# Dynamics buffers given on at the second state step, and a new order of steps on every engine, in a four-layer kernel on one Trainium2 core

## The chip, the cores and the metric

The kernel runs on one core of a Trainium2 chip. The metric is the time of one execution on the device in microseconds (us), all of it: loading the inputs and the weights, the arithmetic and the store of the result. Lower is better. Engines are named as in the profile: PE is TensorE's matmul, PEld its weight load, DVE VectorE, ACT ScalarE, POOL GpSimd, SP SyncE (here it only issues loads).

## The reference, cut to what matters

An input of 8 x 256 tokens of width 128 (float32) goes through four layers. Each layer is a mixer and then a feed-forward stage, each followed by a residual sum and a normalisation:

- layer 0: a complex decaying convolution along the sequence; then 8 experts of which each token uses 2 (hidden width 256)
- layer 1: causal attention with rotary positions (2 heads of 64), with an output projection; then attention with 4 heads on shared keys and values, and 8 + 1 experts (hidden width 128)
- layer 2: attention in a window of 32 (16 heads of 8); then the "dynamics": two iterations of a small state machine, and a refinement
- layer 3: attention of the 32 keys back of which the 16 highest scores count, with a mean over the phrase; then 8 experts (hidden width 342)

The dynamics, to which the change belongs, in short:

```python
probs = softmax(gelu(xf @ router_w1 + b) @ router_w2 + b); topk_p, topk_i = top_k(probs, 2)   # the readout
v, s = 0, xf
for _ in range(2):
    ctx = concat([s, v])
    shared_ctrl = gelu(ctx @ shared_w1) @ shared_w2
    ctrl = for each chosen expert: gelu(ctx @ w1[e]) @ w2[e]
    x_next, v_next = _inl(...)           # sigmoid, softplus, sigmoid of the three parts of the controls
    halt = sigmoid(gelu(s @ halt_w1) @ halt_w2)
    s, v = s + halt * (x_next - s), v + halt * (v_next - v)
out = xf + integration_weight * (gelu(s @ refine_w1) @ refine_w2)        # the refinement
```

## The kernel before

The tokens are cut into four chunks of 512 (two sequences each). Every chunk goes through nine stages: A (convolution), B (experts of layer 0), C, D1 (the two attentions of layer 1), D2 (its experts), E (window attention), F (dynamics), G (phrase attention), H (experts of layer 3). 0F is stage F of chunk 0. A stage is cut into ticks; 0F[12] is its tick 12. Per engine the ticks of one chunk have a fixed order, and the order in which the four chunks' steps are woven together stands in a string of digits per engine (`MERGE`): each digit is the chunk whose next step is written out now. `interleave` reads it. Each engine runs its instructions in the order written and waits on semaphores where it needs another engine's result. A second string, `BANK_OF`, says for each step of PE which of the 8 PSUM banks it writes; before a bank is written again, PE waits for its last reader (`begin`).

What the chunks share is taken in turns (`TURNS`): the `att` buffers (16 tiles of 512 columns, for A, C, D1, E, G), the ring of expert weights and hidden tiles (`w_exp` with 4 slots, `hid` with 6, for B, D2, H), and the `dyn` buffers (16 tiles, for F). For `att` the turns are 0A 1A 2A 3A 0C 0D1 1C 1D1 0E 2C 2D1 1E 3C 3D1 0G 2E 1G 3E 2G 3G; for the ring 0B 1B 0D2 2B 1D2 3B 2D2 3D2 0H 1H 2H 3H; for `dyn` 0F 1F 2F 3F. `take(region, k, stage)` waits for what `released` returns: for `att` after A and D1 the normalisation, else the residual sum; for F too the residual sum, which is its last tick but two (F[55]). So chunk k+1 can't write its first tile of `dyn` before chunk k's refinement is done.

An expert of B takes four 128x512 products on PE (L450, gate and up, two halves) and eight of 128x128 (L485, down); in D2 two and four, in H six and twelve. ACT applies SiLU to the gate (L1820, L1818), DVE multiplies with the up part (L1195, L1192) and adds the weighed result to `x` (L1209, the mix), and only then are the banks free. SP loads the next expert's weights when an older one's down product is done.

Stage F on PE: F[2] and F[4] are the readout (router), F[9] turns the one-hots of the two chosen experts over, F[12] spreads their weights (32 rows), `step(k, n, i)` for n = 0, 1 is a state step: six hidden products (L780), the halt (i = 7, 32 rows), the shared controls (i = 8, L792, 64 rows), eight products that pick the weights of the chosen experts (i = 9 to 12, bf16, 32 rows), the slots' bias (L747, 32 rows) and controls (L757). F[49] to F[54] are the refinement, F[55] to F[57] on DVE and POOL the residual sum and the normalisation. In H, POOL computes a square root by a power (L2180) for the routing.

## Time and profile before

| | us |
|---|---|
| median of 3 runs | 1227.08 |
| lowest, highest | 1224.92, 1227.92 |
| the profiled execution, whole | 1226.56 |
| span of the profiled instructions | 1224.5 |
| PE busy | 1115.4 (91%) |
| DVE, ACT, POOL busy | 827.1, 657.6, 219.1 |
| mean granted clock of PE | 0.959 |

The profile is of one execution. Its times count from the first instruction. In the timeline a row merges instructions of one line that follow each other; on PE a float32 product counts as two. "PEclk" is the granted clock: 1.00 is 2.4 GHz, 0.50 is 1.2 GHz, a mean between them says how much of a stretch lay at either. Two kinds of loss on PE add up: time in which it waits, and time in which it works at half clock.

### The profile page before, as it was taken

The numbers are of one execution on the slowest core, as the hardware profiler recorded it, in microseconds if no ns is written. First come the engines' busy times: TensorE is split into PE (matmuls) and PEld (weight loads), VectorE is DVE, ScalarE is ACT, GpSimd is POOL, SyncE is SP. The second block draws the span as 40 slices with busy tenths as digits, with TensorE's granted clock in tenths as the row PEclk, the third lists the DMA queues.
The fourth block names the chain that finished last, engine by engine and source line by source line (L and its number), as shares of the span: only waits on it lengthen the run. The fifth ranks groups of instructions, "written<-read, shape, count | busy, mean of one in ns | idle before, by whom it ended". The sixth has DMA issues, their size and how long they took to land.

```text
span 1224.5 us, 16730 instructions
## 1 busy us (share of the span) xinstructions
PE 1115.4 (91%) x5800; PEld 629.4 (51%) x5800; DVE 827.1 (68%) x2446; ACT 657.6 (54%) x1028; POOL 219.1 (18%) x251
## 2 busy tenths in 40 slices
PE   0799967799999999999799989999999999999996
PEld 0455544566554455554455555454464553565554
DVE  6987566489577369868486696678584774664534
ACT  0225344555756766677666575668546655542321
POOL 1312042224021214131200150005020000202000
PEclk9899989899989989997899999799999999999999
DMA  7021100121110000001001111001001010111210
GB/s 268 4 73 54 39 14 14 30 68 34 33 48 24 27 14 21 20 27 33 1 14 56 37 37 37 1 18 37 18 28 37 18 37 1 45 36 54 79 56 9
DMA packets 45394, 45.91 MB, mean 37 GB/s; under 512 B 2584, under 2 KB 44192, under 8 KB 45056
## 3 DMA queue, kind: packets, MB, share of 16 engines
q1 hardware_dynamic: 42336, 40.59, 10.9%
q10 hardware_dynamic: 2976, 4.26, 1.0%
q8 instruction: 47, 0.77, 0.2%
q14 instruction: 35, 0.29, 0.1%
HBM read 43.79 MB, written 1.05 MB: 37 GB/s over the span
## 4 chain that ended last, share of the span: by engine, by line
PE 77%; DVE 13%; ACT 4%; DMA 3%; issue 2%; POOL 1%; POOLq 0%; DVEq 0%; ACTq 0%
PE bank L450 32%; PE bank L485 13%; PE bank L757 10%; PE bank L780 5%; ACT L1781 2%; PE bank L457 2%; PE bank L525 2%; PE bank L439 2%; PE bank L747 1%; PE bank L792 1%; PE bank L668 1%; DMA xt<-x_in 1%; DVE x L1209 1%; DMA w_exp<-in_ffn 1%; PE bank L508 1%
## 5 line engine op out<-in xcount | busy, mean ns | idle before, releaser
L450 PE MATMUL bank<-xt,w_exp 128*128 128x512 f32 (+1 forms) x784 | 390.6, 629 | 19.1 <-DMA w_exp<-in_ffn 6.4
L1781 ACT ACT_TABLE_LOAD x186 | 238.6, 1283 | 70.9 <-PE bank L450 41.7
L450 PEld LDWEIGHTS bank<-xt,w_exp 128*128 128x128 f32 (+1 forms) x784 | 134.5, 190 | 193.7 <-issue 117.1
L485 PEld LDWEIGHTS bank<-w_exp,hid 128*128 128x128 f32 (+1 forms) x1568 | 189.3, 196 | 52.2 <-issue 15.8
L485 PE MATMUL bank<-w_exp,hid 128*128 128x128 f32 (+1 forms) x1568 | 199.0, 282 | 5.7 <-DVE hid L1192 4.2
L1209 DVE SCALAR_TENSOR_TENSOR x<-bank,dense,x 128x128 f32<-128x128 f32 x384 | 107.9, 343 | 119.4 <-PE bank L485 103.0
L757 PE MATMUL bank<-picked,w_dyn 128*128 128x512 f32 x320 | 142.9, 596 | 0.0
L1818 ACT ACTIVATE hid<-bank,w_cols 114x512 f32<-114x512 f32 x96 | 65.2, 687 | 114.6 <-PE bank L450 114.0
L2187 POOL TENSOR_SCALAR rstd<-mv 128x4 f32<-128x4 f32 x32 | 7.0, 218 | 552.6 <-DVE mv L1075 552.4
L1820 ACT ACTIVATE hid<-bank 128x512 f32<-128x512 f32 x100 | 57.5, 597 | 85.1 <-PE bank L450 84.7
L757 PEld LDWEIGHTS bank<-picked,w_dyn 128*128 128x128 f32 x320 | 59.1, 190 | 74.8 <-issue 74.7
L2271 POOL TENSOR_TENSOR att<-att,lsm 128x512 f32<-128x512 f32 x64 | 67.8, 1075 | 140.7 <-DVE lsm L1415 130.1
L1192 DVE SCALAR_TENSOR_TENSOR hid<-bank,w_cols,hid 114x512 f32<-114x512 f32 x96 | 70.3, 745 | 27.4 <-PE bank L450 21.1
L1195 DVE TENSOR_TENSOR hid<-bank,hid 128x512 f32<-128x512 f32 x100 | 66.7, 681 | 17.9 <-ACT hid L1820 14.6
L525 PE MATMUL bank<-w_const,att 128*128 128x128 f32 x304 | 45.2, 283 | 12.0 <-DVE hid L1195 3.6
L1844 ACT COPY att<-bank 128x512 f32<-128x512 f32 (+1 forms) x80 | 41.1, 581 | 20.9 <-PE bank L525 20.9
L525 PEld LDWEIGHTS bank<-w_const,att 128*128 128x128 f32 x304 | 35.7, 145 | 30.8 <-issue 12.7
L780 PE MATMUL bank<-xt,w_dyn 128*128 128x512 f32 (+2 forms) x96 | 49.8, 617 | 1.1 <-DVE xt L1531 1.0
L1555 DVE TENSOR_TENSOR picked<-dyn,bank 128x512 f32<-128x512 f32 x64 | 39.5, 679 | 10.3 <-PE bank L450 10.3
L2202 POOL TENSOR_TENSOR att<-att,rowsum 128x512 f32<-128x512 f32 x32 | 32.8, 1051 | 74.5 <-DVE rowsum L1250 74.5
L1793 ACT ACTIVATE xt<-bank 128x512 f32<-128x512 f32 x24 | 14.3, 594 | 58.3 <-PE bank L439 58.3
L1085 DVE TENSOR_SCALAR x<-x,mv,rstd 128x128 f32<-128x128 f32 x112 | 32.5, 353 | 14.3 <-POOL rstd L2188 14.2
(288 smaller groups left out, 1515.9 us busy)
## 6 DMA issues: line engine op xcount, KB each, us to landing
w_exp<-in_ffn SPq DMA_DIRECT2D x68, 192.0 KB, 3.2
w_exp<-in_ffn SPq DMA_DIRECT2D x32, 384.0 KB, 3.5
w_exp<-in_ffn SPq DMA_DIRECT2D x32, 342.0 KB, 3.1
w_dyn<-in_dyn ACTq DMA_DIRECT2D x1, 1636.0 KB, 12.1
w_const<-in_const SPq DMA_DIRECT2D x1, 1274.0 KB, 11.7
xt<-x_in SPq DMA_DIRECT2D x4, 256.0 KB, 15.4
out<-x ACTq DMA_DIRECT2D x4, 256.0 KB, 2.3
att<-in_stage SPq DMA_DIRECT2D x1, 512.0 KB, 5.2
```

Source lines behind the costliest of these rows:

```text
L450: nc.tensor.matmul(seqs(bk[0:rows, :]) if len(rhs.shape) == 3 else bk[0:rows, :], lhsT, rhs, start=True, stop=True).then_inc(S[k % STREAMS ...
L485: last = nc.tensor.matmul(bk[:, t * 128:(t + 1) * 128], hid[0:rows, (e * nf + f) % RING_H, t * 128:(t + 1) * 128], ffn_w(k, st, "down", e, ...
L525: last = nc.tensor.transpose(bk[:, o:o + 128], a(u)[:, i * 128:(i + 1) * 128], ident)
L757: last = nc.tensor.matmul(bk[:], part("dyn", "ex_w2")[:, h * 384 + at:h * 384 + at + 128], picked[:, 2 * h + t - 1, :], start=False, stop= ...
L780: last = nc.tensor.matmul(seqs(bk[0:rows, :]), lhs, src, start=(half == 0), stop=(half == len(use) - 1))
L1192: V.scalar_tensor_tensor(o, u, col("b1", j, rows), o, ALU.add, ALU.mult).then_inc(X.hidden.s, 1)
L1195: V.tensor_tensor(o, u, o, ALU.mult).then_inc(X.hidden.s, 1)
L1209: last = V.scalar_tensor_tensor(x[:, s, t, :], bk[:, t * 128:(t + 1) * 128], dense[:, s, t, ex:ex + 1], x[:, s, t, :], ALU.mult, ALU.add)
L1781: A.preload_act_table_set(name)
L1818: A.activation(dst, src, ACT.Silu, bias=col("bg", j, rows)).then_inc(X.silu.s, 1)
L1820: A.activation(dst, src, ACT.Silu).then_inc(X.silu.s, 1)
L2271: G.tensor_tensor(v, v, spread(lsm[:, u, row, :], 2, 64), op).then_inc(done, 1)
```

## The change

It has two parts.

First, stage F. The readout's hidden tile, the one-hots and the three tiles of the refinement no longer lie in the shared `dyn` buffers but in the chunk's own `nx` (`flat(s)`) and, for the first refinement tile, in its own `xt`. So `take("dyn", k, "F")` moves behind F[4], and the region is given on at the second state step (`X.stepped`), not at the residual sum. The first state step starts one tick later. Since two chunks can now be in F at once, the engines that raise one semaphore for several chunks get a wait for the previous count (`in_turn`, and one on DVE); each is for an earlier instruction of the same engine.

Second, all the digits of `MERGE` and `BANK_OF` are new: the steps of each engine stand in another order. No step is added or taken away; on ACT the new order has 178 table loads among the steps where the old one has 186. `TURNS` and `TICKS` are as they were.

```diff
 MERGE = dict(
     PE=(
-        "0000000100000011200000000003200000000000000000000231111111101000001100111111101010101010111111111111"
...
+        "0000000000000100000000000001001000000002000000220111111111113011111100000110011111100100110101111111"
...
             if u in ("A", "D1"):
                 return S[q].normed, (q, {"A": "a", "D1": "d2"}[u])
+            if u == "F":
+                return X.stepped, (q, 1)
             return S[q].resid, (q, u)
...
-        oh3 = y(F_CTRL)[:, 0:TILES * 3 * 4 * E8].rearrange("p (t r e) -> p t r e", t=TILES, r=3)
+        def one_hots(s):
+            return flat(s)[:, 0:TILES * 3 * 4 * E8].rearrange("p (t r e) -> p t r e", t=TILES, r=3)
+
+        def refining(s, j):
+            return xtv(s) if j else seqs(flat(s))
...
                     if i == 2:
-                        take("dyn", k, "F")
                         pe.wait_ge(T.xt_ready.s, T.xt_ready.at(k, "F"))
...
                     if i == 4:
                         pe.wait_ge(X.ro_hid.s, X.ro_hid.at(k))
-                        by_token(k, ("F", "logits"), lambda t: y(F_VEL)[0:32, t * 128:(t + 1) * 128],
+                        by_token(k, ("F", "logits"), lambda t: flat(s)[0:32, t * 128:(t + 1) * 128],
                                  part("dyn", "ro_w2")[0:32, :], E8, (T.logits, (k, "F")))
                         yield
+                        take("dyn", k, "F")
...
-                    yield from step(k, 0, i - 3, bks)
+                    yield from step(k, 0, i - 4, bks)
...
-                        take("dyn", k, "F")
...
+                        if X.oh_ready.at(k) > 1:
+                            dve.wait_ge(X.oh_ready.s, X.oh_ready.at(k) - 1)
...
+            def in_turn(sg, *event):
+
+                if sg.at(*event) > 1:
+                    act.wait_ge(sg.s, sg.at(*event) - 1)
...
-                        A.activation(y(F_REF + j), T.bank(k, "F", "ref", j)[:], ACT.Gelu,
+                        in_turn(X.ref, k, j)
+                        A.activation(refining(s, j), seqs(T.bank(k, "F", "ref", j)[:]), ACT.Gelu,
```

The lines of the changed kernel lie 5 further on (L450 is L455 there, L485 is L490, L1195 is L1200).

First place, DVE near the start: the convolution of chunk 2 (L1261 to L1280) and what stands around it. Before:

```order
L1195 TENSOR_TENSOR hid<-bank,hid 128x512
L1085 TENSOR_SCALAR x<-bank,mv,rstd 128x128 x4
L1261 TENSOR_TENSOR att<-xt,inject 128x512
L1263 SCALAR_TENSOR_TENSOR att<-sc,att 128x256 x2
L1271 SCALAR_TENSOR_TENSOR att<-sc,att 128x256 x2
L1275 TENSOR_TENSOR att<-att,turn 128x512
L1276 TENSOR_TENSOR att<-xt,att 128x512
L1280 TENSOR_TENSOR att<-att 128x512
L1195 TENSOR_TENSOR hid<-bank,hid 128x512
```

The same place in the changed kernel, again from the end of chunk 1's stage A on:

```order
L1200 TENSOR_TENSOR hid<-bank,hid 128x512 x2
L1090 TENSOR_SCALAR x<-bank,mv,rstd 128x128 x4
L1266 TENSOR_TENSOR att<-xt,inject 128x512
L1268 SCALAR_TENSOR_TENSOR att<-sc,att 128x256 x2
L1214 SCALAR_TENSOR_TENSOR x<-bank,dense,x 128x128 x4
L1200 TENSOR_TENSOR hid<-bank,hid 128x512 x2
L1276 SCALAR_TENSOR_TENSOR att<-sc,att 128x256 x2
L1280 TENSOR_TENSOR att<-att,turn 128x512
L1281 TENSOR_TENSOR att<-xt,att 128x512
```

What moved: expert work of chunk 0 (hidden tiles and a mix) now stands between the two halves of chunk 2's scans, and the end of chunk 3's stage A stands behind all of 0B and behind six hidden tiles of 1B, where before only half of 0B stood ahead of it.

Second place, PE in the first state step of chunk 2's dynamics (2F), from its shared controls (L792) to its slot bias. Before:

```order
L792 MATMUL bank<-dyn,w_dyn 128x512 x2
L450 MATMUL bank<-kt,w_const 128x512 x2
L450 MATMUL bank<-ohb,slot_b 128x512 x8
L450 MATMUL bank<-xt,w_exp 114x512
L747 MATMUL bank<-kt,w_dyn 128x512 x2
L450 MATMUL bank<-xt,w_exp 114x512 x2
```

In the changed kernel:

```order
L797 MATMUL bank<-dyn,w_dyn 128x512 x2
L455 MATMUL bank<-xt,w_exp 114x512
L455 MATMUL bank<-ohb,slot_b 128x512
L455 MATMUL bank<-xt,w_exp 114x512
L455 MATMUL bank<-ohb,slot_b 128x512
L455 MATMUL bank<-xt,w_exp 114x512
L455 MATMUL bank<-ohb,slot_b 128x512 x2
L455 MATMUL bank<-xt,w_exp 114x512
L455 MATMUL bank<-ohb,slot_b 128x512
L455 MATMUL bank<-xt,w_exp 114x512
```

What moved: the eight picking products (`ohb,slot_b`, 32 rows) stood in one block; now full-height products of 0H stand between them.

Third place, PE near the end: the last product of 3G (`att`) and the start of 3H. Before:

```order
L935 MATMUL bank<-att 128x128
L450 MATMUL bank<-xt,w_exp 114x512 x6
L485 MATMUL bank<-w_exp,hid 128x128 x12
L439 MATMUL bank<-w_const,x 128x128 x4
L949 MATMUL bank<-sc,w_const 128x8
L450 MATMUL bank<-xt,w_exp 114x512
L457 MATMUL bank<-w_rows,xt 128x8 x4
L450 MATMUL bank<-xt,w_exp 114x512 x5
L485 MATMUL bank<-w_exp,hid 128x128 x12
```

In the changed kernel:

```order
L940 MATMUL bank<-att 128x128
L490 MATMUL bank<-w_exp,hid 128x128 x12
L974 MATMUL bank<-w_b,nx 128x128 x4
L444 MATMUL bank<-w_const,x 128x128 x4
L954 MATMUL bank<-sc,w_const 128x8
L462 MATMUL bank<-w_rows,xt 128x8 x4
L455 MATMUL bank<-xt,w_exp 114x512 x12
L490 MATMUL bank<-w_exp,hid 128x128 x12
```

What moved: between 3G's last product and 3H's turning over (L439, now L444) stood half an expert's six products and twelve down products, and then five experts of 2H before 3H's own experts; now it is the last down products of 2H and the bias product, and 3H follows at once.

## Rows read from the trace of the kernel before

**Rows 1.** The page: busy time of each engine.
```profile
PE 1115.4 (91%) x5800; PEld 629.4 (51%) x5800; DVE 827.1 (68%) x2446; ACT 657.6 (54%) x1028; POOL 219.1 (18%) x251
```
**Rows 2.** Stretches: start:end, length, busy (x instructions), granted clock, DMA share, GB/s.
```profile
0.00:104.50 104.50, 65.59 (x271) 39.27 (x271) 84.80 (x293) 23.02 (x34) 21.13 (x25) 0.97 0.33 109
104.50:170.20 65.70, 57.96 (x363) 37.83 (x363) 41.36 (x141) 34.34 (x84) 18.26 (x26) 1.00 0.13 37
170.20:248.40 78.20, 59.21 (x321) 36.68 (x321) 43.78 (x156) 34.00 (x85) 19.38 (x29) 0.89 0.09 28
248.40:1146.70 898.30, 864.42 (x4549) 477.39 (x4549) 622.86 (x1755) 546.46 (x797) 157.96 (x168) 0.96 0.10 30
1146.70:1224.50 77.80, 68.24 (x300) 38.27 (x300) 34.33 (x104) 19.73 (x28) 2.40 (x4) 0.97 0.14 42
```
**Rows 3.** Timeline of PE, 34 to 80 us: start, length, idle before and releaser.
```profile
34.65 1.84 PE L457 MATMUL bank<-w_lat,xt 128*128 128x8 f32 x8 [0.84 <-ACT xt L1793]
...
49.48 1.03 PE L457 MATMUL bank<-w_lat,xt 128*128 128x8 f32 x8 [0.78 <-ACT xt L1793]
55.03 1.12 PE L439 MATMUL bank<-w_const,att 128*128 128x128 f32 x4 [4.52 <-DVE att L1280]
...
76.17 2.04 PE L485 MATMUL bank<-w_exp,hid 128*128 128x128 f32 x16
78.06 3.76 PE L450 MATMUL bank<-xt,w_exp 128*128 128x512 f32 x8
...
104.49 3.67 PE L450 MATMUL bank<-xt,w_att 128*128 128x512 f32 x8
```
**Rows 4.** Timeline of DVE, 32 to 47 us: stage A of chunk 1, a router, a hidden tile.
```profile
32.70 0.69 DVE L1261 TENSOR_TENSOR att<-xt,inject 128x512 f32<-128x512 f32 x1
...
40.05 0.18 DVE L1144 COPY small<-bank 128x32 f32<-128x32 f32 x1
...
43.25 0.88 DVE L1072 BATCH_NORM_STATS2 stats<-bank 128x6 f32<-128x128 f32 x4
44.17 0.38 DVE L1075 BATCH_NORM_AGGREGATE mv<-stats 128x2 f32<-128x6 f32 x4
44.47 0.66 DVE L1195 TENSOR_TENSOR hid<-bank,hid 128x512 f32<-128x512 f32 x1
46.04 1.37 DVE L1085 TENSOR_SCALAR x<-bank,mv,rstd 128x128 f32<-128x128 f32 x4 [0.91 <-POOL rstd L2188]
```
**Rows 5.** Timeline of PE in 1D1, 222 to 250 us.
```profile
225.56 1.66 PE L450 MATMUL bank<-xt,w_exp 128*128 128x512 f32 x2 [2.44 <-ACT att L1835]
...
246.89 1.06 PE L554 MATMUL bank<-w_lat,att 128*128 128x128 f32 x8
248.37 1.95 PE L450 MATMUL bank<-xt,w_exp 128*128 128x512 f32 x4 [0.42 <-DVE x L1209]
```
**Rows 6.** Stretches at half clock inside F of chunks 0 to 3, columns as in rows 2.
```profile
335.20:342.00 6.80, 6.80 (x14) 2.91 (x13) 1.88 (x3) 3.96 (x6) 0.00 (x0) 0.50 0.00 0
567.30:581.00 13.70, 11.90 (x40) 5.29 (x41) 10.94 (x24) 10.75 (x23) 5.24 (x6) 0.50 0.00 0
775.60:792.70 17.10, 17.10 (x26) 4.99 (x25) 8.08 (x13) 8.46 (x11) 0.00 (x0) 0.50 0.01 1
963.30:966.70 3.40, 3.40 (x6) 1.41 (x5) 3.17 (x6) 0.95 (x1) 0.00 (x0) 0.50 0.00 0
```
**Rows 7.** Timeline of PE in 2F, 774 to 787 us.
```profile
774.94 3.21 PE L792 MATMUL bank<-dyn,w_dyn 64*128 64x512 f32 x4
778.07 3.78 PE L450 MATMUL bank<-kt,w_const 32*128 32x512 f32 x4
781.65 3.88 PE L450 MATMUL bank<-ohb,slot_b 32*128 32x512 bf16 x8
```
**Rows 8.** Timeline of PE, 600 to 611 us: 3D1's projection, then 0G.
```profile
600.95 1.05 PE L554 MATMUL bank<-w_lat,att 128*128 128x128 f32 x8
608.49 2.08 PE L876 MATMUL bank<-w_const,x 128*128 128x128 f32 x8 [6.48 <-DVE nx L1096]
```
**Rows 9.** Timeline, all engines, 1105 to 1118 us: from 3G to the start of 3H.
```profile
1105.30 1.12 DVE L1680 SCALAR_TENSOR_TENSOR x<-bank,small,x 128x128 f32<-128x128 f32 x4 [1.29 <-PE bank L935]
...
1109.77 1.10 DVE L1085 TENSOR_SCALAR x<-x,mv,rstd 128x128 f32<-128x128 f32 x4
...
1110.87 2.94 PE L485 MATMUL bank<-w_exp,hid 114*128 114x128 f32 x24
...
1117.31 5.42 POOL L2180 TENSOR_TENSOR small<-small,expo 128x32 f32<-128x32 f32 x1 [8.19 <-DVE small L1711]
```
**Rows 10.** Timeline of PE, 1142 to 1147 us: the end of 2H.
```profile
1142.47 2.92 PE L485 MATMUL bank<-w_exp,hid 114*128 114x128 f32 x24 [1.97 <-DVE hid L1192]
1145.31 1.15 PE L969 MATMUL bank<-w_b,nx 8*128 8x128 f32 x8
```

100 lines of the change are left out of this document (50 added, 50 removed).

## The prediction

> **What bounds the kernel now.** Read the page's busy line first [rows 1]: PE is busy in 91% of the span, DVE in 68%, ACT in 54%. PE is what everything else feeds, so the question is never how long an instruction on DVE or ACT takes, but whether PE has something to do meanwhile, and at which clock. Then the stretches [rows 2]. Up to 104.5 us PE is busy for 65.6: 27 us pass before its first product can start, and some 12 more in waits. From 104.5 to 170.2 it idles 7.7 us, from 170.2 to 248.4 it idles 19.0 us at a mean clock of 0.89. The long middle, 898 us, has 33.9 us of idle time, under 4%. The last 78 us are chunk 3's experts alone. So a new order can win in three places: the first 250 us, the half clock, and a few single waits; the middle leaves little.
>
> **Part one, stage F's buffers.** It removes no instruction. The waits it adds are for an earlier instruction of the same engine, which is done long before; I cost them at nothing, and they would cost at most 16 times the 0.1 us or so that lies between dependent DVE rows [rows 4], under 2 us. What it gives is freedom: the readout of chunk k+1 can run beside the end of chunk k. In the trace of before no wait on PE for the `dyn` buffers is seen, since the old order put experts there. So this part alone is worth nothing; it counts through the order that it permits.
>
> **Part two, the start.** Before, DVE does all four stages A almost in one piece, and PE waits for chunk 2's at 50.5 us, 4.52 us long, beside 0.84 and 0.78 and two smaller ones: about 7 us, and 6.8 us at half clock after it, 3.4 us lost [rows 3]. In the new order PE has twelve steps of 0B before chunk 1's A, and the DVE work of 0B stands between the scans. This wait goes. But what does the chain of attentions gain? 0C may not touch `att` before 3A is normalised. DVE's sum up to there in the new order: 32.6 us (the end of 0A's scaling, just before the group's first row), then three stages A of 7.35 + 1.26 + 1.37 = 10.0 us each [rows 4], three routers of 3.2, weights 2.5, 22 hidden tiles of 0.65, nine mixes of 1.1 and one normalisation of 2.4: 30.0 + 9.6 + 2.5 + 14.3 + 9.9 + 2.4 = 68.7, together 101.3, with small waits 103. PE's own sum to the same point: from 35.5 us 47 products of 0.9 and ten down groups of 1.9 [rows 3], 42.3 + 19.0, and 8 for transposes, routers and stalls, gives 105. Both say that 0C's projections start at 105 us, and today they start at 104.49 [rows 3]. The chain gains nothing at the start. PE is ahead by some 8 us of 1B, but 1B is also what fills 0D1, so at the end of 0D1 both kernels have done the same work: gain about 1 us, from the SiLU of 1B which no longer comes between 0D1's exponentials on ACT, against one router that now does on DVE.
>
> Next, 1D1. Before, nine experts of 0D2 are all that PE can weave in, and it idles between its products: 2.44 us at 225.6, and so on, until 2B starts at 248.37 [rows 5]. In the new order 0D2 is finished earlier and eleven steps of 2B stand before 1D1's projection: ten products of 0.9 and one down group of 1.9, 10.9 us [rows 3]. They have 19.0 us of idle time to go into [rows 2]. From there on PE is nearly full, so what it is ahead it keeps. **Start: -11 us**, between 0 (the chain becomes later by as much) and -19 (all the idle time of the stretch goes).
>
> **Part two, the clock.** Inside the first state step of F, PE falls to half clock in all four chunks: 6.8, 13.7, 17.1 and 3.4 us, 41.0 in all [rows 6], and half of such a time is lost if PE would have had work, 20.5 us. In the longest one PE was busy throughout [rows 6]; what it did before and in it were products of 64 and 32 rows, one after the other for 10.6 us [rows 7]. In the new order 2F's picks alternate one by one with full-height products of 0H, and 1F's partly with 2D2; 0F's and 3F's blocks stay nearly whole. If the spells of 1F and 2F shrink from 30.8 to about 12 us, 9 us come back. **Clock: -9 us**, between 0 and -20.
>
> Here a rule speaks against me. The row shows a fall without any idle time before it [rows 6]. The Trainium skill, "TensorE: Matmul & The Clock Gate", section "HAM oscillation — how this bites in real kernels", tells of falls that come after PE has idled; by it alone the order of F's products would change nothing, and the sum would be 9 us higher. I go with the row.
>
> **Part two, single waits.** 0G waits 6.48 us for 3D1's last normalisation [rows 8]. The new order puts four steps of 2D2 ahead of it, 3.6 us, and 3D2's transposes. **-4 us**, between 0 and -6.5.
>
> **Part two, the end.** Before, 41 us of 2H follow 3G's last product, from 1105.2 to the first product of 3H behind the row of 1145.31. In the new order only 2H's last down group (2.9) and bias product (1.15) [rows 10] stand between it and 3H. The chain from T, the end of 3G's product: residual sum and statistics 2.4, then on DVE first 2H's mix and sum (which wait for PE, to T + 4.9), scaling 1.1, transposes 0.6, ACT 0.6, logits 1.0: 3H's first product at T + 8.4, in place of T + 5.5 by PE's own work, 2.9 us idle. Then 3H's router waits for POOL's power of 5.42 us [rows 9] on DVE, and five hidden tiles queue behind it; PE can write six halves ahead (10.4 us) before its first down group needs them at T + 20: 2 to 3 us more, and a spell at half clock, 1.7. Against that, today's wait of 1.97 [rows 10] goes. **End: +6 us**, between +1 and +15 (if banks stop PE sooner).
>
> **The middle.** 33.9 us of idle time less 0G's; the new order has other waits. I see no reason for a balance either way: 0, give or take 10. ACT's eight table loads less are 10 us of an engine that is half idle, 0 on PE.
>
> Sum: -11 - 9 - 4 + 6 = -18 from the profiled execution's 1226.6 gives 1208.6; the median of the runs lies 0.5 above that execution, so 1209.
>
> **The rivals.** (a) The clock stays: the spells only move, as idle time elsewhere brings new ones. For it: the stretch with the most idle time, 19.0 of 78.2 us, also has the lowest clock, 0.89 [rows 2], so idle time costs clock as well. 1209 + 9 = 1218. (b) The chain is late: DVE reaches the end of 3A later than 103 us. For it: my sum has it fully busy for 70 us, in fixed order. Each microsecond is one on the attention chain until 1D1; at 114 us the first term is gone, 1220. (c) The orders are equal in what they cover and only the places of the waits change; part one does nothing: 1225. (d) The middle gets better by a third of its idle time too: 1198. (e) **Slower:** the weaving is too fine. The new PE order has 704 rows of equal instructions in place of 649, 55 more changes from one chunk to another; each one that finds its bank still held by a DVE step (0.66 us, the hidden tile) [rows 4] costs PE that much. If more than 33 of them do (18 + 3.7 over 0.66) the kernel is slower than before; if all do, 1245. For it: 8 banks, and eight of them held by a stage D1's scores. Against it: DVE is idle in a third of the span [rows 1], and today's waits of this kind are few.
>
> **How the numbers follow.** The forecast 0.42, (a) 0.16, (b) 0.12, (c) 0.08, (d) 0.10, (e) 0.12. The predicted time is the forecast's, 1209. The range from 1195 to 1230 holds the forecast with its bounds, (a), (b), (c), (d) and the light end of (e). A measurement of this kernel can tell about 0.3% (3.7 us) from no change. Faster than 1223.4: the forecast, (a), (b) and (d) nearly whole, 0.78; within 0.3%: most of (c) and some of (a) and (b), 0.10; slower: (e), 0.12.
>
> **What the new profile would show.** Start: no wait of PE near 50 us; 0C's projections between 103 and 107; 2B's first products before 1D1's projection; at 250 us PE busy 11 us more. Clock: no spell of over 7 us in 2F's picks, and a mean granted clock of 0.965 or more. 0G's wait under 4 us. End: a wait of PE of about 3 us after 2H's bias product and another near 3H's first down group, so that the time from 3G's last product to the end is some 90 us, where PE's work and the end of the chain make 82 (2.9 + 1.15 + 77.8). The prediction is wrong if the first 104 us keep their idle time, if 0C starts after 110, if the spells of 2F are as long as before, or if PE's idle time from 250 us on differs from 34 us by more than 12.

## The result, and the profile after

The changed kernel takes **1222.2 us** in the median of 8 runs (1216.9 to 1228.5) against 1227.0 for the kernel before: ratio 0.9963, 95% interval 0.9947 to 0.998. Measured once more beside other kernels it gave 0.9954 (0.9933 to 0.9976). So it is faster, by 0.4%; the forecast was 1.5% (1209 us). The sign was right and the size was not.

The execution that was profiled took 1227.4 us, one of the slowest of the eight; its mean granted clock is 0.946, while the eight runs lie between 0.944 and 0.954 and their time follows the clock. One profile of this kernel is therefore a poor witness of its clock. In what follows two sums are kept apart, each a mean over all runs of a kernel: **half-clock loss** = span times (1 - mean granted clock), and **the rest** = span times mean clock, which is what the span would be if nothing ran at half clock. The loss is an upper bound, since half clock during idle time costs nothing.

The page, and the five stretches that answer [rows 1] and [rows 2]. Three of the ends are moved to the same places in the program: the last projection of 0D1, the end of 1D1 and the start of 3H (here 3H's router; its first expert product comes at 1143.68). The first end is left at 104.5, although 0C's first projection now comes at 109.89. Columns: start:end, length, busy time of PE, PEld, DVE, ACT, POOL, granted clock, DMA share, GB/s.

```profile
PE 1126.8 (92%) x5800; PEld 631.7 (52%) x5800; DVE 825.7 (67%) x2446; ACT 646.2 (53%) x1020; POOL 219.0 (18%) x251
```
```profile
0.00:104.50 104.50, 67.64 (x287) 40.29 (x287) 82.34 (x287) 23.12 (x34) 19.91 (x23) 0.98 0.33 110
104.50:173.70 69.20, 60.90 (x351) 39.01 (x351) 42.86 (x151) 31.97 (x83) 19.60 (x28) 0.88 0.12 34
173.70:256.60 82.90, 65.87 (x357) 40.88 (x358) 49.59 (x177) 42.06 (x95) 20.36 (x30) 0.92 0.11 32
256.60:1142.00 885.40, 858.28 (x4500) 469.28 (x4500) 614.26 (x1715) 529.36 (x780) 150.10 (x163) 0.95 0.10 30
1142.00:1225.60 83.60, 74.09 (x308) 42.29 (x308) 36.62 (x119) 19.72 (x28) 9.05 (x7) 0.91 0.12 36
```

PE's idle time fell from 109.1 us (1224.5 less 1115.4) to 98.8, by 10.3. But PE's busy time rose by 11.4 us for the same 5800 instructions, while the mean granted clock of the profiled executions fell from 0.959 to 0.946: they ran at half clock more often.

Where a wait is due to what, summed over the trace: the waits of PE for an expert's weights that are still on their way (`w_exp`) are the largest group behind the start (11.5 us; 6.4 us in the kernel before).

```profile
PE bank L455 <- DMA w_exp<-in_ffn: 11.5, 5, 2.9
PE bank L455 <- DVE x L1214: 6.5, 6, 3.2
PE bank L444 <- DVE x L1090: 6.4, 2, 4.3
PE bank L455 <- DVE nx L1101: 5.4, 1, 5.4
```

The columns are total us, times, longest. Here the first three of the five waits for weights stand in the timeline of PE; they lie just where the prediction had put its gain of the start, in 0D2 and ahead of 1D1's first product (218.93, `nx`):

```profile
204.50 1.12 PE L455 MATMUL bank<-xt,w_exp 128*128 128x512 f32 x2 [1.46 <-DMA w_exp<-in_ffn]
211.25 1.99 PE L455 MATMUL bank<-xt,w_exp 128*128 128x512 f32 x4 [2.92 <-DMA w_exp<-in_ffn]
217.06 2.08 PE L455 MATMUL bank<-xt,w_exp 128*128 128x512 f32 x2 [2.84 <-DMA w_exp<-in_ffn]
218.93 1.06 PE L444 MATMUL bank<-w_const,nx 128*128 128x128 f32 x4
```

The stretches at half clock of 0D1 and 1C's start, and those in the first state steps of 0F to 3F, against [rows 6]:

```profile
155.60:172.70 17.10, 12.11 (x68) 7.46 (x66) 7.46 (x34) 9.70 (x31) 8.03 (x8) 0.50 0.01 1
176.10:186.30 10.20, 6.09 (x7) 2.43 (x8) 4.15 (x14) 0.00 (x0) 3.22 (x5) 0.50 0.00 0
343.30:346.70 3.40, 3.40 (x5) 1.51 (x5) 1.65 (x3) 3.39 (x15) 0.00 (x0) 0.50 0.01 2
350.10:356.90 6.80, 5.97 (x16) 3.69 (x17) 2.71 (x6) 1.78 (x4) 2.92 (x7) 0.50 0.02 7
548.10:565.20 17.10, 16.21 (x30) 6.50 (x31) 11.31 (x24) 5.54 (x14) 4.07 (x4) 0.50 0.04 12
766.60:780.30 13.70, 13.70 (x18) 2.83 (x16) 5.13 (x10) 6.46 (x8) 1.20 (x2) 0.50 0.00 1
933.80:944.00 10.20, 10.20 (x17) 3.19 (x15) 7.77 (x13) 6.65 (x8) 0.00 (x0) 0.50 0.00 0
```

And PE in 2F, where the prediction expected the alternation to help, against [rows 7]: the picks (`ohb,slot_b`) do alternate with full-height products of 0H, PE waits for nothing, and it still is at half clock from 766.6 to 780.3 (a product of L455, two instructions, takes 2.05 us in place of 1.11). The clock falls inside the shared controls (L797), 3.6 us before the first pick starts at 770.20.

```profile
765.51 2.77 PE L797 MATMUL bank<-dyn,w_dyn 64*128 64x512 f32 x4
768.21 2.05 PE L455 MATMUL bank<-xt,w_exp 128*114 128x512 f32 x2
770.20 0.60 PE L455 MATMUL bank<-ohb,slot_b 32*128 32x512 bf16 x1
770.73 2.05 PE L455 MATMUL bank<-xt,w_exp 128*114 128x512 f32 x2
...
780.81 1.11 PE L455 MATMUL bank<-xt,w_exp 128*114 128x512 f32 x2
```

The spell doesn't come each time. Of the six profiles with this order of PE in 2F and few-row products there (the changed kernel's two, the one with the old start, the two with extra products in 0D1, the one with deep weights, all below), four have 13.7 us at half clock here and two have none. In the deep-weights kernel the same products in the same order ran at full clock:

```profile
753.40:767.10 13.70, 13.70 (x43) 5.42 (x43) 9.76 (x24) 9.01 (x12) 1.20 (x2) 1.00 0.14 41
```
```profile
755.03 1.98 PE L822 MATMUL bank<-dyn,w_dyn 64*128 64x512 f32 x4
756.95 1.11 PE L480 MATMUL bank<-xt,w_exp 128*114 128x512 f32 x2
757.99 0.39 PE L480 MATMUL bank<-ohb,slot_b 32*128 32x512 bf16 x1
```

### The profile page after: what moved, and what is told of

Its sections match the earlier page's. It is cut to its first block, busy times and chain, and to the rows that moved or that the text cites. A ratio compares the mean times of both kernels' runs of the same rounds, so it can differ in the third digit from the quotient of the medians.

```text
span 1225.6 us, 16722 instructions
## 1 busy us (share of the span) xinstructions
PE 1126.8 (92%) x5800; PEld 631.7 (52%) x5800; DVE 825.7 (67%) x2446; ACT 646.2 (53%) x1020; POOL 219.0 (18%) x251
## 4 chain that ended last, share of the span: by engine, by line
PE 82%; DVE 9%; ACT 4%; DMA 3%; issue 2%; POOL 0%; POOLq 0%; DVEq 0%; ACTq 0%
PE bank L455 34%; PE bank L490 14%; PE bank L762 11%; PE bank L785 4%; PE bank L462 2%; PE bank L530 2%; ACT L1787 2%; PE bank L444 2%; PE bank L752 2%; PE bank L797 1%; DVE x L1214 1%; DMA xt<-x_in 1%; DMA w_exp<-in_ffn 1%; PE bank L673 1%; PE bank L550 1%
## 5 line engine op out<-in xcount | busy, mean ns | idle before, releaser
L455 PE MATMUL bank<-xt,w_exp 128*128 128x512 f32 (+1 forms) x784 | 402.0, 641 | 21.0 <-DMA w_exp<-in_ffn 11.5
L455 PEld LDWEIGHTS bank<-xt,w_exp 128*128 128x128 f32 (+1 forms) x784 | 137.5, 195 | 194.2 <-issue 121.8
L490 PEld LDWEIGHTS bank<-w_exp,hid 128*128 128x128 f32 (+1 forms) x1568 | 188.8, 195 | 51.8 <-issue 17.8
L490 PE MATMUL bank<-w_exp,hid 128*128 128x128 f32 (+1 forms) x1568 | 198.8, 281 | 7.3 <-DVE hid L1200 3.6
L762 PE MATMUL bank<-picked,w_dyn 128*128 128x512 f32 x320 | 147.2, 606 | 0.0
L1200 DVE TENSOR_TENSOR hid<-bank,hid 128x512 f32<-128x512 f32 x100 | 66.9, 684 | 23.8 <-ACT hid L1826 18.2
L2004 ACT ACTIVATE dyn<-bank 128x512 f32<-128x512 f32 x16 | 9.5, 597 | 78.4 <-PE bank L762 78.4
## 6 DMA issues: line engine op xcount, KB each, us to landing
w_dyn<-in_dyn ACTq DMA_DIRECT2D x1, 1636.0 KB, 11.8
w_const<-in_const SPq DMA_DIRECT2D x1, 1274.0 KB, 11.5
```

The source lines that it names most:

```text
L455: nc.tensor.matmul(seqs(bk[0:rows, :]) if len(rhs.shape) == 3 else bk[0:rows, :], lhsT, rhs, start=True, stop=True).then_inc(S[k % STREAMS ...
L490: last = nc.tensor.matmul(bk[:, t * 128:(t + 1) * 128], hid[0:rows, (e * nf + f) % RING_H, t * 128:(t + 1) * 128], ffn_w(k, st, "down", e, ...
L762: last = nc.tensor.matmul(bk[:], part("dyn", "ex_w2")[:, h * 384 + at:h * 384 + at + 128], picked[:, 2 * h + t - 1, :], start=False, stop= ...
L1200: V.tensor_tensor(o, u, o, ALU.mult).then_inc(X.hidden.s, 1)
```

## The experiments

All ratios are to the kernel before, measured beside each. "Before" and "changed" are the two kernels of this study; "deep weights" is explained under "Weights on their way".

| kernel | median us | ratio (95% interval) | mean clock (median) | half-clock loss | rest |
|---|---|---|---|---|---|
| changed (second measurement) | 1222.8 | 0.9954 (0.9933-0.9976) | 0.951 | 60.0 | 1160.8 |
| part one alone | 1227.7 | 0.9986 (0.9969-1.0003) | 0.955 | 55.6 | 1170.3 |
| changed, old start | 1226.0 | 0.9966 (0.9947-0.9984) | 0.954 | 56.7 | 1166.4 |
| changed, all rows full | 1211.6 | 0.9845 (0.9818-0.9872) | 0.969 | 36.8 | 1172.0 |
| before, all rows full | 1221.2 | 0.9927 (0.9901-0.9952) | 0.968 | 35.2 | 1183.8 |
| changed, rows full but the controls' and the halt's | 1217.6 | 0.9913 (0.9890-0.9936) | 0.968 | 37.7 | 1177.9 |
| all rows full, old start | 1213.9 | 0.9888 (0.9865-0.9912) | 0.971 | 36.4 | 1175.6 |
| changed, deep weights | 1206.3 | 0.9827 (0.9807-0.9846) | 0.959 | 48.4 | 1156.1 |
| before, deep weights | 1219.3 | 0.9923 (0.9896-0.9950) | 0.960 | 49.5 | 1167.6 |
| changed, deep weights, all rows full | 1205.9 | 0.9827 (0.9810-0.9845) | 0.968 | 37.1 | 1166.5 |
| changed, rows full but the bias' | 1193.3 | 0.9742 (0.9723-0.9761) | 0.973 | 32.2 | 1160.2 |
| changed, deep weights, rows full but the bias' | **1188.2** | **0.9666** (0.9643-0.9689) | 0.974 | 30.1 | 1155.4 |
| the same, old start | 1192.7 | 0.9715 (0.9693-0.9737) | 0.973 | 34.1 | 1157.2 |
| before, deep weights, rows full but the bias' | 1206.4 | 0.9837 (0.9823-0.9850) | 0.971 | 37.1 | 1167.5 |

The kernel before itself, beside the first row: 1228.4 us, loss 55.0, rest 1171.4. With 5 to 17 runs a kernel, the difference of two losses is known to some 3 to 6 us (95%), that of two rests to 1 to 3 us.

### Part one alone

The changed stage F (its buffers, its release at the second state step), with the tables of the kernel before; the first state step keeps its old place so that those tables still fit:

```
-                    yield from step(k, 0, i - 4, bks)
+                    yield from step(k, 0, i - 3, bks)
```

> The changed kernel's stage F (its readout and refinement in each chunk's own buffers, the shared ones given on at the second state step, eight fewer loads of ACT tables), but in the orders of the kernel before. The prediction costs part one at nothing: then this run takes what the kernel before takes, 1223 to 1231 us, and the whole difference of the changed kernel is its order. Rival: part one has a worth of its own (fewer waits for the shared buffers, fewer table loads on ACT): 2 us or more faster, 1224 or less, with less idle time on PE in the stretches of F. Third: its added waits cost up to 2 us: 1229 or more.

Measured: 1227.7, 0.9986. The interval holds 1: part one is worth nothing by itself, as costed. All of the gain is the order. The expectation's "eight fewer loads of ACT tables" is wrong for this run: its profile has 186 table loads, as the kernel before. The eight loads less belong to the new order, and what they are worth was not tried.

### Few-row products and the clock

In F the products of 32 and 64 rows are widened to 128 rows; what is added is zeros in the weights or in the input, so the result stays. Two examples, the bias and the halt:

```
-                    rows = slice(32 * r, 32 * r + 32)
+                    rows = slice(0, 128)
...
-                    whole(k, ("F", n, "halted"), part("dyn", "ha_w2")[0:32, :], y(F_HALT)[0:32, :], 128,
+                    whole(k, ("F", n, "halted"), part("dyn", "ha_w2"), y(F_HALT), 128,
```

> The changed kernel, in which every product of stage F that used 64 or 32 rows of TensorE (the halted and the shared controls, the one-hot products, the picks and the slot's bias) uses all 128 rows, the added ones with zeros as weights or as input; number, order and columns of the products are the same, and so are the other engines' steps. Theory of the prediction: products of few rows pull the clock down. Then the spells at half clock in F (51.2 us in the first state steps, some 20 in the later ones) mostly go, the mean granted clock rises from 0.95 to 0.97 or more and the time falls by 15 to 30 us against the changed kernel, to 1192 to 1207. Rival: the rows don't matter, the clock falls for idle time or by chance: the same spells at the same places, mean clock within 0.004, time within 4 us of the changed kernel.

> The same edit on the kernel before: all of F's products of 64 or 32 rows made full. If rows set the clock, its 41.0 us of half clock in the first state steps of F go, and it gains up to 20 us: 1205 to 1215; and since both kernels then have no such spells, the new one's lead on the old one at full rows is what its order saves in idle time, some 10 to 15 us. If rows don't matter, 1223 to 1231.

Measured: 1211.6 (0.9845) and 1221.2 (0.9927): the mean clock rose, to 0.969 and 0.968, but the time fell less than expected; both kernels missed their ranges (1192 to 1207 and 1205 to 1215), and the lead of the new order is 9.6 us. The stretch from 250 to 1100 us of the changed kernel's two profiles, and of the one with full rows (columns as above):

```profile
250.00:1100.00 850.00, 825.56 (x4345) 446.87 (x4343) 588.77 (x1628) 518.37 (x764) 148.90 (x161) 0.95 0.10 28
```
```profile
250.00:1100.00 850.00, 823.94 (x4372) 446.40 (x4372) 589.62 (x1629) 521.17 (x767) 148.91 (x161) 0.96 0.10 28
```
```profile
250.00:1100.00 850.00, 820.50 (x4428) 463.26 (x4430) 598.59 (x1664) 524.87 (x774) 148.96 (x161) 0.99 0.10 29
```

So products with few rows do bring the clock down while PE is busy, though not each time; with the same number of products and zeros in the other rows the stretch is at 0.99. The loss falls from 60 to 37 us in the new order and from 55 to 35 in the old one. But the rest grew by 11 to 12 us in both, so that only 11 and 7 us of time came back. The groups of PE instructions by line show why: first the slot's bias at 32 rows (changed kernel), then at 128.

```profile
L752 PE MATMUL bank<-kt,w_dyn 32*128 32x512 f32 x80 | 21.3, 739 | 0.4 <-DVE x L1214 0.4
```
```profile
L752 PE MATMUL bank<-kt,w_dyn 128*128 128x512 f32 x80 | 37.6, 600 | 0.4 <-DVE x L1217 0.4
```

Eighty instructions (40 products) of 739 ns take 21.3 us together: they use rows 0 to 31, 32 to 63 and 64 to 95 and run side by side. At full rows they run one after the other, 37.6 us. The Trainium skill ("TensorE: Matmul & The Clock Gate", Part 3: Packing small matmuls — row/col tiling) says that products in distinct row groups overlap; these rows agree.

To see which few-row products matter, the halted product and the shared controls got their 32 and 64 rows back:

> The changed kernel with only F's products of 32 rows made full (the one-hot products, the picks and the slot's bias); the shared controls keep 64 rows and the halted product 32. With all of them full the spells at half clock in F's first state steps went and the kernel took 0.9845 of the kernel before. If the picks alone do it (they are the longest rows of such products), the ratio is 0.985 to 0.988 (1210 to 1214 us) with no spell over 3.4 us at the picks; if it takes the 64-row products that come just ahead too, spells of 6.8 us stay there and the ratio is 0.989 to 0.994 (1215 to 1221).

Measured: 1217.6, 0.9913, 6 us slower than with all rows full. The time is the second case's, but no spell of 6.8 us stands at the picks: in 2F there is none. The loss hardly changed (37.7), the rest did (1177.9 against 1172.0). Of these 6 us 3.0 stand in the group of the controls, L797, 21.6 us at 64 rows and 18.6 at 128 in the two profiles; where the others lie is open. So most of the clock came back with the 32-row products. As the run below keeps the bias at 32 rows, it is the picks and the spread weights (`kt,w_const`) that matter most; these two were not parted. The controls are not free of it: in this profile half clock begins in the controls of 3F's second state step, where six instructions take 5.19 us (2.84 in the kernel before at full clock), with no wait.

```profile
996.29 5.19 PE L797 MATMUL bank<-dyn,w_dyn 64*128 64x512 f32 x6
```

With full rows except at the bias, where they cost concurrency:

> The changed kernel with full rows in F except for the slot's bias, weights placed as in the changed kernel. With deep weights this edit took 1.6 per cent off. If the two edits are independent, 0.9958 less 0.016: 0.977 to 0.983, 1200 to 1208 us, and the mean clock 0.965 or more; if part of what each gives is the same half clock, more than that: 0.974 to 0.977.

Measured: 1193.3, 0.9742, the stronger of the two cases. Loss 32.2 in place of 60.0, rest 1160.2 where the changed kernel has 1160.8: 28 us of loss went, and all of it became time. The bias group in this kernel, still with 32 rows:

```profile
L752 PE MATMUL bank<-kt,w_dyn 32*128 32x512 f32 x80 | 18.1, 640 | 0.4 <-DVE x L1217 0.4
```

### Idle time and the clock in 0D1

Two trials put 26 extra full-height products, whose result is overwritten, into the waits of 0D1 and ahead of 1C's first projection; each is written into the bank that the waiting product has opened (the shorter form is shown, the first trial had all 512 columns):

```
+                for _ in range(FILL.get(opens[0], 0)):
+                    nc.tensor.matmul(banks[i][:, 0:256], ident, part("const", "window")[:, 0:256], start=True, stop=True)
```

> The changed kernel with 26 extra full-height products (identity times a constant of 512 columns, 0.43 us each at full clock), put where PE waits in 0D1 and ahead of 1C's first projection: each is written into the bank that the waiting product opens, before its operands are waited for, and then overwritten. They fill 12.9 us of waits. If idle time is what brings the clock down there, the 27.3 us at half clock between 155 and 187 us go, 0.4 to 0.5 of that is won, less what idle time it lay beside: 4 to 9 us, to 1213 to 1219 us. Rival one: the chip makes up for it later, the mean clock stays within 0.003 and the time within 2 us of 1222 to 1224. Rival two: the extra products delay the real ones, 1226 or more.

> The changed kernel with 26 extra products as in the first trial (same places, same counts), but of 256 columns, half as long: 26 times 0.43 us in 12.9 us of waits. The first trial took 1.0045 of the kernel before; its extra products took some 22 us in 12.9 us of waits, so that 9 to 10 us of its loss is delay. If idle time at 0D1 costs clock (27.3 us at half clock there in the changed kernel, 3.4 in the first trial), this run is 3 to 8 us faster than the changed kernel: ratio 0.990 to 0.994. If the clock that is saved there is lost later (the first trial's other runs had a mean clock of 0.950 to 0.959, as without the products), it is within 0.2 per cent of 0.9963.

Measured: 1233.1 (1.0045) with 512 columns, the second rival's case, and 1227.7 (0.9999) with 256, outside both cases. The first was mis-sized: an f32 product of 512 columns is two instructions and takes 0.86 us, not 0.43. The second fits the waits. From 150 to 190 us, changed kernel and the one with short products:

```profile
150.00:190.00 40.00, 25.69 (x148) 15.81 (x146) 18.09 (x66) 15.41 (x46) 13.60 (x15) 0.66 0.00 1
```
```profile
150.00:190.00 40.00, 31.87 (x213) 24.12 (x208) 19.21 (x71) 16.10 (x49) 13.62 (x15) 0.96 0.00 1
```

So here the clock falls for want of work in the waits: with the waits filled it stays at 0.96. (0D1's own products are small too; how much of the fall is theirs was not tried apart.) The Trainium skill ("TensorE: Matmul & The Clock Gate", "HAM oscillation — how this bites in real kernels") has falls follow idle time, and at 0D1 the trace agrees; in 2F, where PE waited for nothing, it does not. And yet the time rose by 5 us. Over all runs of the short-product kernel the loss is 59.0 us, as in the changed kernel (60.0): what was kept in 0D1 went elsewhere. Where to can't be told: its profile has a spell of 23.9 us in 1F, but there the changed kernel's own two profiles differ as much (17.1 and 3.4). The rest rose from 1160.8 to 1166.2; most likely the extra products delay the real ones where a wait is shorter than in the profile that the counts come from, which was not tried apart. The 27.3 us at half clock in 0D1, which I took for a loss of some 9 us, could not be turned into time, and the kernel that was fastest of all still has them: much of them is idle time (17.10 - 12.11 and 10.20 - 6.09 in the rows above, 9.1 us), and most likely the chain of DVE, ACT and POOL sets the pace there; that was not shown apart.

The same on top of the faster forms:

> The changed kernel with all of F's products at full rows and with 98 extra full-height products in nearly all waits of PE of 0.5 us or more from 80 us on (0D1 and 1C, the waits for experts' weights at 200 to 215, 346 and 583 us, 2D1, 3H's start, the last down group). In the full-row kernel 73 us were at half clock, next to idle time. If idle time brings it down, most of the 61 us ahead of the last 8 go and the time falls by 10 to 22 us below the full-row kernel's 1211.6: 1190 to 1202 us, mean clock 0.985 or more. If the spells come by themselves, 1208 to 1215.

> The one before it, with 45 short extra products (identity times 256 columns of a constant) in the waits of 0D1, of 1C's first projection, of 2D1, of 3H's start and of the last down group. The first trial with such products had them twice as long as the waits (each took 0.86 us, not 0.43) and so lost what it won; these are meant to end within the waits. If idle time brings the clock down, the 20 us of half clock in 0D1 and the 17 of 3H go and it is 5 to 15 us faster than without them: 1187 to 1197 us. If not, 1198 to 1206 us, or slower by as much as the waits are shorter than in the profile that the counts come from.

Measured: 1254.5 (1.0208) with 98 of the long kind, which delay PE by more than they save although the mean clock is 0.988; 1206.0 (0.9818) with 45 short ones, against 1205.9 (0.9827) for the same kernel without them. In the latter the loss fell from 37.1 to 21.2 us and the rest rose from 1166.5 to 1182.3: nothing is won. In none of the four trials did keeping PE warm with work of no use win time.

### The start

> The changed kernel, but the first some 200 us in the orders of before (a prefix of the four engines' orders that holds the same steps in both); from there on the new orders. Theory: the new start was to give 11 us and gave 3.4 us less idle time at 250 us, while PE is at half clock for 27.3 us of 0D1 and 1C, where before it was for 6.8 to 10; that is a loss of some 9 us against a gain of 3.4. Then the old start is 3 to 8 us faster than the changed kernel, 1214 to 1219 us, with no spell at half clock over 7 us between 140 and 190 us. Rival one: the half clock only moves elsewhere (the chip gives back what it took): the mean granted clock stays within 0.003 of the changed kernel's and the time is 1222 to 1228. Rival two: the start is worth what was forecast and without it the kernel is slower: 1230 or more.

Measured: 1226.0, 0.9966, the changed kernel within 0.1%; the first rival's case. In the kernel as it is, the new start is worth nothing that can be measured. With full rows:

> All of F's products at full rows, and the first some 200 us in the orders of before. In the changed kernel itself the old start made no difference (0.9966 against 0.9963 of the kernel before), where 3.4 us less idle time stand against more half clock. With F's clock out of the way: if the new start is worth its idle time, this run is 2 to 5 us slower than the full-row kernel with the new start (1214 to 1217 us); if the two cancel as before, it is within 2 us of it (1210 to 1213.5).

Measured: 1213.9, 0.9888 against 0.9845: 5 us.

### Weights on their way

Each expert's weights went into one of four slots of 1068 columns, although an expert of D2 has 384. Now they are laid one behind the other by their size in the same buffer, and a load waits only for the experts whose place it takes:

```
-                slot = n % RING_W
-                if n >= RING_W:
-                    q, u, v = EXPERTS[n - RING_W]
+                slot = n % LANDS
+                at0, held = PLACES[n]
+                for m in sorted(last.values()):
+                    q, u, v = EXPERTS[m]
                     sp.wait_ge(S[q].filled, S[q].full(q, u, "down", v))
-                to = w_exp[:, slot, :]
+                to = w_exp[:, at0:at0 + SIZE[st]]
```

> The changed kernel, with the experts' weights placed in the same buffer by their real size (384 columns for one of D2 in place of a slot of 1068), so that up to eleven of D2's experts fit where four did, and each load waits only for the experts whose place it takes. In the changed kernel PE waits for weights on their way (w_exp) at 204.5, 211.3, 217.1, 350.9 and 597.2 us, 1.46 + 2.92 + 2.84 + 1.39 + 2.91 = 11.5 us, where before it was 6.3. The prediction's first term (11 us at the start, of which 3.4 came) had no place for this. If it is the cause, the waits go and the time falls by 6 to 12 us against the changed kernel, to 0.987 to 0.991 of the kernel before (1212 to 1217 us), with PE's idle time at 250 us at 55 to 58 in place of 62.2. Rival: the products then wait at the same place for something else (1D1's chain): idle time at 250 us above 60, and the time within 3 us of the changed kernel's.

> The kernel before with the deeper placement of weights. It waits 6.3 us for weights, the changed kernel 11.5. If the changed kernel's gain was held back by weights, this run gains clearly less than the changed kernel did (1.4 per cent): ratio 0.992 to 0.997, 1219 to 1225 us, and the new order is then 10 to 16 us faster than the old one, about as forecast. If weights held both orders back alike, the ratio is 0.985 to 0.988 and the new order's lead stays at 0.3 to 0.5 per cent.

Measured: 1206.3 (0.9827) in the new order, more than expected, and 1219.3 (0.9923) in the old one, the case in which the changed kernel was held back by weights. PE's waits in 0D2 now:

```profile
204.23 1.10 PE L480 MATMUL bank<-xt,w_exp 128*128 128x512 f32 x2 [0.88 <-ACT hid L1851]
209.55 1.96 PE L480 MATMUL bank<-xt,w_exp 128*128 128x512 f32 x4 [1.46 <-DVE x L1239]
214.40 1.10 PE L480 MATMUL bank<-xt,w_exp 128*128 128x512 f32 x2 [1.91 <-DVE hid L1225]
```

No wait for weights is left, but 4.3 of the 7.2 us have turned into waits for ACT and DVE: PE's idle time up to 250 us is 59.6 us, not the 55 to 58 expected (62.2 in the changed kernel). Of the 16 us won, 4 to 5 are in the rest and 12 in the clock. The old order won 4 and 6. So the weights held back the new order more, 1.3% against 0.8%. How they cost clock is not shown. In the profiles the half clock beside the three waits of 0D2 is gone (3.4 us in one profile of the changed kernel, 6.8 in the other), but so are the 13.7 us of 2F, where no wait for weights stands; that spell is also missing in the first trial with extra products, whose weights are placed as before. So part of these 12 us may be a shift in time of what runs when.

> The same placement of weights, and all of F's products at full rows: both causes of lost time at once. If they add, 0.9845 less 0.5 to 1.0 per cent: ratio 0.975 to 0.980, 1198 to 1204 us; if the waits for weights only hide others, 1208 to 1213 us.

Measured: 1205.9, 0.9827: with all rows full the two edits did not add; the time is below both cases. That led to the bias:

> The changed kernel with the deeper placement of weights and full rows in F, except for the products of the slot's bias, which keep their 32 rows: there three row groups work side by side, and the 80 products took 21.3 us in the changed kernel and 37.6 at full rows. Full rows with all of them gave 0.9827 together with deep weights, no more than deep weights alone. If the lost concurrency ate the clock's gain, this run is 10 to 16 us faster than that: ratio 0.969 to 0.975, 1191 to 1198 us. If the bias products pull the clock down as the others do, the half clock comes back and the ratio stays at 0.980 to 0.984.

> The one before it with the first some 200 us in the orders of before. With weights and F's clock out of the way, the new start can show its worth: the prediction gave it 11 us (then 0.978 to 0.984), the full-row pair without deep weights showed 0.4 per cent, 5 us (then 0.973 to 0.979). If it was held back by weights alone, this run is 8 to 11 us slower than the one before it; if the chain of attentions sets the time to 250 us in both, 2 to 5 us.

> The kernel before with the deeper placement of weights and full rows in F except for the slot's bias: the pair to the fastest kernel so far (0.9666), which has the new orders. Forecast of the new order's lead, without its clock term: 9 us, 0.75 per cent; with the clock term 18 us, 1.5 per cent. If the order's lead is what the pair with deep weights shows (1.0 per cent), this run is at 0.974 to 0.979, 1197 to 1203 us; if the new order was also held back by F's clock, at 0.980 to 0.986; if the lead is used up, at 0.966 to 0.970.

> The changed kernel as it is, beside the three others on the same chip: 0.9963 of the kernel before as measured first, give or take 0.002; the mean clock of its runs 0.944 to 0.954. Outside 0.994 to 0.999 the comparisons of the earlier runs with its first measurement have to be read again.

Measured: 1188.2 (0.9666), 1192.7 (0.9715), 1206.4 (0.9837) and 1222.8 (0.9954). The bias' concurrency was worth 18 us, more than expected. The first of these beats both kernels, by 3.3 and 2.9%. The old start costs it 4.5 us, the case in which the chain of attentions sets the time to 250 us in both. Its pair with the old orders is 18 us behind, the case named "the new order was also held back by F's clock". The stretch from 250 to 1100 us of the fastest kernel:

```profile
250.00:1100.00 850.00, 821.88 (x4509) 464.02 (x4509) 610.74 (x1700) 528.08 (x779) 149.18 (x163) 0.99 0.10 30
```

## Why the prediction was wrong

The new order against the old one, in four forms of the kernel (differences of the table's rows, new less old, us):

| form | rest | half-clock loss | together |
|---|---|---|---|
| as they are | -10.6 | +5.0 | -5.6 |
| deep weights | -11.5 | -1.1 | -12.6 |
| deep weights, rows full but the bias' | -12.1 | -7.0 | -19.1 |
| all rows full | -11.8 | +1.6 | -10.2 |
| forecast | -9 | -9 | -18 |

**The step that failed is the clock**, -9 in the sum. It was +5.0, give or take 3. Its mechanism was right in part: PE falls to half clock in F while it is busy, because of products with few rows, and the spells there mostly go when their rows are filled. What was wrong is the cure and its size. I took it that alternation with full-height products would shrink the spells of 1F and 2F from 30.8 to about 12 us. The alternation came as foreseen. The spells sum to 30.8 and 17.1 us in the two profiles of the changed kernel, and over the six profiles with this order and few-row products they lie anywhere between 3.4 and 37.6, 20.5 in the mean, against 30.8, 30.8 and 23.9 in three profiles of the old order. So it gave perhaps 4 us of the 9, and not reliably.

One reason stands in the rows already. The prediction says of 2F's spell that "what it did before and in it were products of 64 and 32 rows, one after the other for 10.6 us". But that block starts at 774.94 [rows 7] and the spell at 775.60 [rows 6]: nearly all of the block is in the spell and not ahead of it, and the picks start only at 781.65. In the changed kernel too the clock fell before the first pick. Picks that alternate come too late to prevent that fall.

And half clock came up elsewhere, most of all at the end. There the prediction set 1.7 us for a spell at 3H's start. From 1100 us to the end, first the kernel before, then the changed kernel's two profiles:

```profile
1100.00:1224.50 124.50, 112.74 (x526) 66.10 (x524) 55.48 (x171) 28.57 (x41) 9.02 (x7) 0.98 0.16 49
1100.00:1225.60 125.60, 113.42 (x525) 69.13 (x524) 65.76 (x217) 32.93 (x50) 10.25 (x9) 0.94 0.14 42
1100.00:1219.50 119.50, 107.35 (x497) 67.37 (x496) 64.32 (x214) 29.44 (x44) 10.26 (x9) 0.92 0.15 44
```

The clock of 0.98 against 0.94 and 0.92 is 5 to 7 us more of half-clock loss in this stretch, as much as the whole +5.0. The changed kernel has 6.8 and 10.2 us at half clock around 3H's start, the place where 2H no longer stands between 3G and 3H and PE waits 2.0 us; the kernel before has none there. Rival (a), which was given 0.16, is nearest: it said that idle time elsewhere brings new spells. (3.4 of the 10.2 us begin before that wait, so idle time is not the whole of it.)

The placement of the weights matters as well: with deep weights the loss falls by 11.6 us in the new order and by 5.5 in the old one. With deep weights alone the two orders have the same loss, within the noise; with full rows as well the new one has 7 us less, and then the sum reaches the forecast's -18. That is no confirmation of the forecast: it takes two edits that the prediction did not have, and the pair with full rows but without deep weights was measured in the new order only.

**The rest of the sum was right in total, -9 against -10.6, but not in its parts.**

- Start, -11: the term was more than three times too large. PE's idle time at 250 us fell by 3.4 (65.6 to 62.2), and the start taken alone is worth nothing in the changed kernel and 5 us in the fastest. The failed piece is "They have 19.0 us of idle time to go into": that stretch, 4.7 us longer now, still has 17.0 us of it (82.90 - 65.87). 2B's steps stand where they were announced, but the ring of four slots gave the experts around them their weights late, 7.2 us, and behind those waits stood others. Of the first 104 us only part came as computed: the wait of 4.52 us of [rows 3] is gone, PE is busy for 67.6 us in place of 65.6, but 3.25 and 1.06 us of new waits stand at 85 to 90 us and 0C's first projection comes at 109.9, where 103 to 107 were named and 104.49 was before.
- 0G, -4: its wait of 6.48 us is gone; 2.91 us for weights stand just ahead of it instead. Net -3.6.

```profile
597.18 1.13 PE L455 MATMUL bank<-xt,w_exp 128*128 128x512 f32 x2 [2.91 <-DMA w_exp<-in_ffn]
598.14 0.60 PE L444 MATMUL bank<-w_const,nx 128*128 128x128 f32 x4
598.58 1.06 PE L881 MATMUL bank<-w_const,x 128*128 128x128 f32 x8
```

- End, +6: from the last product of 3G (T = 1134.53) to the end of the span 91.1 us, where 90 were forecast. The chain against [rows 9] and [rows 10]: 3H's transposes at T + 6.0 with 2.01 us of idle time, its router 0.66 more. 3H's first expert product is at T + 9.15, where 8.4 was forecast. The second wait, 2 to 3 us near the first down group, did not come; the half clock of above took its place, so that the total fits partly by luck.

```profile
1134.53 2.94 PE L490 MATMUL bank<-w_exp,hid 114*128 114x128 f32 x24
1134.71 1.13 DVE L1686 SCALAR_TENSOR_TENSOR x<-bank,small,x 128x128 f32<-128x128 f32 x4 [1.74 <-PE bank L940]
...
1139.40 1.11 DVE L1090 TENSOR_SCALAR x<-x,mv,rstd 128x128 f32<-128x128 f32 x4
...
1140.57 0.66 PE L444 MATMUL bank<-w_const,x 128*128 128x128 f32 x4 [2.01 <-DVE x L1090]
...
1142.01 1.83 PE L462 MATMUL bank<-w_rows,xt 128*128 128x8 f32 x8 [0.66 <-ACT xt L1799]
```

- The middle, 0 give or take 10: PE's idle time behind 250 us is 36.6 us (98.8 - 62.2), 6.9 less than the 43.5 of before (109.1 - 65.6). The "34" of the prediction's last part left out the end, so that test was set at the wrong number.
- Part one, 0: shown by its own run.

Rival (e), too fine weaving, would have made the kernel slower by new waits for banks; it is excluded, since idle time fell. What stays open is why the same products bring the clock down in one profile and not in another, and what in a few-row product the clock goes by. With all rows full the two orders' losses differ by +1.6 in place of +5.0 us; that change is smaller than the scatter of the runs.

## What to carry to other kernels

When a new order fills PE's waits, look in the old trace for what becomes the next wait, and count transfers among it: here a ring of weights that cost the old order 9 us cost the new one 16, and with it more than half of its lead (5.6 us in place of 12.6). When PE falls to half clock without waiting, look at the rows of its products, and fill them with zeros where they run alone, but not where several row groups run side by side. And before paying for a warm clock in a stretch, ask whether PE sets the pace there; here no such work won time.

## What the runs showed of the hardware

- Filling few-row products (all but the bias') with zeros to 128 rows took the mean clock from 0.951 to 0.973 and 2.1% of the kernel before's time off, with not one product less. The forty instructions of the 64-row controls (L797) took 21.2 us, at full rows 18.6; most of the difference is half clock (four of them took 1.98 us at full clock and 2.77 in 2F's spell).
- The same few-row products in the same order were at half clock for 13.7 us in four profiles and at full clock in two.
- Products of 32 rows in three row groups overlap: 80 instructions in 18.1 us at 640 ns each, against 37.6 us at full rows.
- The same kernel, run again, has a mean clock of 0.944 to 0.955 and a time of 1216.9 to 1228.5 us; its two profiles show 51.2 and 27.3 us of half clock in the first state steps of F (two rows of the second below). A clock effect of 1% can't be read from a single profile.

```profile
547.60:551.00 3.40, 3.40 (x5) 0.60 (x3) 3.37 (x8) 2.86 (x5) 2.20 (x3) 0.50 0.00 0
759.20:772.90 13.70, 13.70 (x18) 3.06 (x16) 5.35 (x14) 6.46 (x8) 1.21 (x2) 0.50 0.00 1
```
